# Attention's two shorter high halves of the probabilities: from ScalarE to GpSimd

## The reference

```python
x = x + 0.5 * _L0_ffn_ref(_layernorm(x), ...)
x = x + _L0_attn_ref(_layernorm(x), w_q, w_kv, w_dense)
x = x + 0.5 * _L0_ffn_ref(_layernorm(x), ...)
# _L0_attn_ref, the part that matters here:
scores = jnp.einsum('bqgpd,bkgd->bgqpk', q, k) * SCALE
scores = jnp.where(causal, scores, -jnp.inf)
probs = jax.nn.softmax(scores, axis=-1)
ctx = jnp.einsum('bgqpk,bkgd->bqgpd', probs, v)
return jnp.einsum('bse,eh->bsh', ctx, w_dense)
```

## Time and profile before

| | us |
|---|---|
| median of 3 runs | 2606.5 (2606.39 to 2609.38) |
| profiled execution | 2606.3 |
| its span | 2604.5 |
| TensorE busy in the span | 2512.5 (96%) |
| VectorE busy | 2151.8 (83%) |
| ScalarE busy | 945.6 (36%) |
| GpSimd busy | 909.6 (35%) |

### The profile page before, as it was taken

The page is one execution under the profiler, slowest core; times in us unless marked ns, Lnnn a source line. Parts: engine busy times, 40 slices in busy tenths (PEclk is TensorE's granted clock), DMA queues, the critical chain, the costliest instruction groups (busy, mean ns, idle before and its releaser), DMA issues. The chain is left out here.

```text
span 2604.5 us, 45222 instructions
## 1 busy us (share of the span) xinstructions
PE 2512.5 (96%) x14116; PEld 2298.7 (88%) x14116; DVE 2151.8 (83%) x6164; ACT 945.6 (36%) x2546; POOL 909.6 (35%) x1950
## 2 busy tenths in 40 slices
PE   6999999999997999999999999997999999999998
PEld 6999999999995888888888888886899999999997
DVE  6888888888886888888888888886888888888887
ACT  3111111101103777777777777774101101101100
POOL 4332332332323434343434344334332322323321
PEclk9999999999998999999999999998999999999999
DMA  6000000000001554554545554555000000000000
GB/s 191 13 1 1 1 1 1 1 1 1 1 25 50 91 91 92 92 92 92 89 90 88 90 92 92 89 96 136 25 9 1 9 9 1 9 9 1 9 9 9
DMA packets 378736, 117.25 MB, mean 45 GB/s; under 512 B 338561, under 2 KB 377473, under 8 KB 378497
## 3 DMA queue, kind: packets, MB, share of 16 engines
q1 hardware_dynamic: 378496, 114.36, 22.0%
HBM read 26.24 MB, written 4.19 MB: 12 GB/s over the span
## 5 line engine op out<-in xcount | busy, mean ns | idle before, releaser
L555 PE MATMUL ffn_ring<-ffn_mix_weights,ffn_yT 128*128 128x384 f32 x5760 | 1157.2, 342 | 5.9 <-DVE ffn_mix_weights L790 3.4
L555 PEld LDWEIGHTS ffn_ring<-ffn_mix_weights,ffn_yT 128*128 128x128 f32 x5760 | 1009.1, 190 | 56.7 <-DVE ffn_mix_sums L725 15.8
L727 DVE SCALAR_TENSOR_TENSOR ffn_mix_sums<-ffn_ring,ffn_w,ffn_mix_sums 128x384 f32<-128x384 f32 x896 | 550.6, 615 | 244.1 <-PE ffn_ring L555 227.5
L605 PE MATMUL ffn_ring<-ffn_out_weights,ffn_avT 128*128 128x512 f32 x1536 | 442.9, 399 | 6.3 <-POOL ffn_avT L1028 4.5
L1547 ACT ACTIVATE attn_exponentials<-attn_exponentials,attn_score_neg_max 128x512 f32<-128x512 f32 (+3 forms) x512 | 285.7, 559 | 164.3 <-DVE attn_score_neg_max L1462 163.7
L1615 POOL CAST attn_probsT_long<-attn_turned_long 128x1024 fp32r<-128x1024 f16 (+1 forms) x256 | 232.5, 936 | 251.1 <-DVE attn_probs L1479 250.4
L605 PEld LDWEIGHTS ffn_ring<-ffn_out_weights,ffn_avT 128*128 128x128 f32 x1536 | 283.0, 189 | 36.2 <-POOL ffn_avT L1028 5.7
L1479 DVE SCALAR_TENSOR_TENSOR attn_probs<-attn_exponentials,attn_prob_factor,attn_probs 128x512 f16<-128x512 f32 (+3 forms) x512 | 248.2, 546 | 15.5 <-ACT attn_probs L1556 15.2
L1556 ACT ACTIVATE attn_probs<-attn_exponentials,attn_prob_factor 128x512 f16<-128x512 f32 (+3 forms) x512 | 250.0, 552 | 23.1 <-DVE attn_prob_factor L1472 15.6
L742 DVE SCALAR_TENSOR_TENSOR x<-ffn_ring,ffn_w_out,x 128x256 f32<-128x256 f32 x512 | 247.1, 483 | 13.0 <-PE ffn_ring L605 6.5
L1302 PE MATMUL attn_scores<-attn_kT,attn_qT 128*128 128x512 f32 (+2 forms) x1152 | 242.8, 338 | 4.7 <-DVE attn_qT L1445 3.2
(11 more groups left out here) (149 smaller groups left out, 3262.4 us busy)
## 6 DMA issues: line engine op xcount, KB each, us to landing
ffn_mix_stage<-in_L_ffn_q_proj_dram SPq DMA_DIRECT2D x32, 128.0 KB, 2.5
ffn_mix_stage<-in_L_ffn_k_proj_dram SPq DMA_DIRECT2D x32, 128.0 KB, 2.5
ffn_mix_stage<-in_L_ffn_v_proj_dram SPq DMA_DIRECT2D x32, 128.0 KB, 2.8
ffn_out_stage<-in_L_ffn_o_proj_dram SPq DMA_DIRECT2D x16, 256.0 KB, 2.9
out_dram<-x SPq DMA_DIRECT2D x8, 512.0 KB, 2.9
x<-in_L_attn_x_dram SPq DMA_DIRECT2D x7, 512.0 KB, 8.3
early_stage<-in_L_attn_w_q_dram SPq DMA_DIRECT2D x4, 512.0 KB, 5.2
attn_dense_stage<-in_L_attn_w_dense_dram SPq DMA_DIRECT2D x4, 512.0 KB, 4.8
```

The costliest lines, as they stand in the source:

```text
L555: last = pe.matmul(bank[:, 0:QKV], yT[:, t % 2, h, k * P:(k + 1) * P], mix_half(e, wh)[:, k], start=(n == 0), stop=(n == 3 * CK - 1))
L605: last = pe.matmul(bank[:], avT[:, t % 2, h], wo[:, g, wh], start=(i == 0), stop=(i == 2))
L727: dve.scalar_tensor_tensor(into, bank[:, 0:QKV], w[:, t, e:e + 1], into, ALU.mult, ALU.add).then_inc(mix_done, 1)
```

## The change

GpSimd gets a function that makes the high halves of the blocks 1 and 0 of the unit before, and calls it at the head of its slot, ahead of its wait for the low halves and of its casts. ScalarE keeps the blocks 3 and 2. The semaphore that counted high halves becomes two, one for each engine, and VectorE's low halves wait for the one of their block. The wait for the landed short transpose goes to GpSimd together with the work.

```diff
-        p_hi, p_lo = sem("prob_hi"), sem("prob_lo")
+        p_hi_long, p_hi_short, p_lo = sem("prob_hi_long"), sem("prob_hi_short"), sem("prob_lo")
...
             def split_probs(u, i):
                 _, h, n = u
-                dve.wait_ge(p_hi, done_of(n, i))
+                dve.wait_ge(p_hi_long if pair_of(i) else p_hi_short, 2 * n + 2 - i % 2)
...
                 act.activation(prob_half(0, i), expo[:, at:at + width].rearrange("p (j k) -> p j k", k=P), ACT.Copy,
-                               scale=p_factor[:, h % 2, i:i + 1]).then_inc(p_hi, 1)
+                               scale=p_factor[:, h % 2, i:i + 1]).then_inc(p_hi_long, 1)
...
                 if prev:
-                    for i in reversed(range(QT)):
-                        split_probs(prev, i)
+                    split_probs(prev, 3)
+                    split_probs(prev, 2)
...
+            def split_short_probs(u, i):
+                _, h, n = u
+                pool.wait_ge(r_done, 4 * n + 4 - i // 2 * 2)
+
+                reach(pool, t_landed[pair_of(i)], 16 * n)
+                at, width = PROB_AT[i], (i + 1) * P
+                pool.tensor_scalar(prob_half(0, i), expo[:, at:at + width].rearrange("p (j k) -> p j k", k=P),
+                                   p_factor[:, h % 2, i:i + 1], None, ALU.mult).then_inc(p_hi_short, 1)
...
             def slot(b, h):
+                prev = unit(b, h, 1)
+                if prev:
+                    split_short_probs(prev, 1)
+                    split_short_probs(prev, 0)
```

## The result

The changed kernel takes 2660.7 us in the median of five runs (2654.96 to 2663.77) against 2606.4 us of the kernel before in the same session: a ratio of 1.0205, 95% interval 1.0194 to 1.0216. That is slower by 54 us where 31 were forecast. It lies inside the range of 2613 to 2666 us that the chances were given for, but above the 2618 to 2658 us that the forecast's own steps allowed, in the stretch that rival (a) claimed. The profiled execution took 2661.75 us, its span 2659.7.

The account below looks back on a forecast made before the run. TensorE was taken to bound the attention stage, VectorE second. ScalarE's relief counted nothing; VectorE's 0.45 us loss per head reached TensorE as 31 us, so 2606.3 + 31 = 2637 us, own range 2618 to 2658, overall 2613 to 2666.

Parts of the forecast that it names:

- (a): GpSimd kept out until VectorE's two long low halves are done; d of 0.6 to 0.8 us, 2650 to 2667 us; chance 0.17.
- Part 1: ScalarE losing two rows per head, about 0.8 us, only lengthens its idle time: worth nothing; upper bound 14.8 us.
- Part 2: GpSimd's two new operations at its slot's head take about 0.54 and 0.43 us, with their data in time.
- Part 3: GpSimd's reads collide with VectorE's two-input low halves; VectorE loses each operation's length less 0.25 us, d = 0.45 us.
- d: VectorE's loss per head in the attention stage: 0.45 us, low end 0.19, high end 0.70.
- Part 4: VectorE's lateness reaches TensorE at dense in slots without enough margin: 4.1 us per item, 31 us in all.
- (b): Port held for the whole of GpSimd's operation: d = 0.97 us, some 10 us per item, 2683 us; chance 0.03.
- (c): No difference: port holds so brief that margins and idle swallow them; 2606 us, 2603 to 2611; chance 0.09.
- (d): Faster: no real collision, ScalarE's relief brings forward high halves VectorE waits for; 8 us, 2598 us; chance 0.04.
- The signs that I gave: Low halves grow 0.45 us per head (384-wide and 128-wide); TensorE's wait 29 to about 60 us; ScalarE's up 0.8 us.

Follow-up runs that it names:

- e5: Changed kernel, but ScalarE keeps block 1 and GpSimd makes only block 0's high half (128 columns): 2616.2 us, 1.0038.
- e6: Changed kernel with GpSimd copying the exponentials instead of scaling them, factor left out of the short high halves: 2619.0 us, 1.0054.
- e2: Kernel before, ScalarE making all four high halves, plus GpSimd doing the two new operations into a buffer nobody reads: 2625.7 us, 1.0068.
- e9: Changed kernel with GpSimd filling the short high halves with zeros, three fills each, reading nothing from SBUF: 2656.4 us, 1.0189.
- e11: Changed kernel with GpSimd's layer norm power moved behind the two short high halves of the next slot: 2656.6 us, 1.0190.
- e4: Changed kernel with ScalarE also making the two short high halves, into a spare buffer: 2658.3 us, 1.0195.
- e10: Changed kernel with GpSimd filling the short high halves with zeros, five and three fills, no SBUF reads: 2744.3 us, 1.0528.
- e7: Changed kernel with VectorE's maxima of block 3 moved between its second and third low halves: 2632.8 us, 1.0101.
- e1: Kernel before with nobody making the two short high halves, so ScalarE is relieved and GpSimd gets nothing: 2606.05 us, 0.9997.
- e3: Kernel before with GpSimd making four constant fills of a spare buffer at the slot's head, reading nothing: 2607.0 us, 0.9998.
- e8: Kernel before, but ScalarE scales the two short blocks in place and GpSimd makes both their high and low halves: 2596.5 us, 0.9965.

## Why the prediction was right in kind and short in size

**One curve for these runs.** The time goes with the burst's mean length, whether the burst is lengthened by the port or by lateness:

```
run                 burst us  longer by  time us   more   us per us
e5 one block          2.073     0.133    2616.2    10.1      76
e6 copies             2.124     0.184    2619.0    12.8      70
e2 port alone         2.212     0.272    2625.7    19.7      72
e9 fills              2.488     0.548    2656.4    49.7      91
e11 power behind      2.512     0.572    2656.6    49.9      87
e4 ScalarE busy       2.522     0.582    2658.3    52.3      90
changed kernel        2.547     0.607    2660.7    54.3      89
e10 more fills        3.208     1.268    2744.3   137.7     109
```

e9 has no read in its high halves and costs about as much per us as e4 and e11: the changed kernel needs no large cause beyond its longer burst. The agreement is not a proof, because e9's lateness lies differently over the slots (3.3 us in slot 9, 2.2 in slots 1, 2 and 13). By the intervals e2's price is 49 to 81 us per us and the changed kernel's 83 to 93, so the price does rise; e5 and e6 are too uncertain to be ranked. e10's 109 contains the lower clock: less my estimate of 29 us it is 86, no more than the four runs at 0.55 to 0.61. (e7's burst has the maxima inside and can't be compared.)

**Part 1 (the relief is worth nothing): right,** e1 and e4.

**Part 2 (0.54 and 0.43 us, data in time): wrong,** the step that failed. Undisturbed the operations take 0.92 and 0.60 us. The slope between them, (922 - 602) / 128 = 2.5 ns per column, is three times that of the casts from which I had extrapolated. e6's copies of the same blocks (0.40 and 0.29 us) show that the operation makes the difference, not the data: a multiplication by a per-row scalar is not a cast. 0.92 us alone would still have been in time (e9, slots 3 and 5 to 8). What I left out is that the hold works both ways: I priced GpSimd's hold on VectorE, but "undisturbed" was wrong of GpSimd, which starts 0.18 us behind VectorE and loses some 0.42 us to its first low half. The earlier trace rows had that too, 1.11 us for 0.735. The sum, 0.18 + 1.35 = 1.53 us, passes the 1.2 us at which the third low half is due. Together with the overlap between instructions that a gap takes away, with slots 9 to 12 and with the four late transposes, this lateness makes the 0.607 of the changed kernel out of e2's 0.272.

**Part 3 (the collision, d = 0.45): mechanism right, its terms wrong, the sum in its range.** GpSimd did get in after the first of the back-to-back low halves in most heads. But VectorE did not lose GpSimd's duration less 0.25 us, which would be 0.67 and 0.35 us. It lost 0.22 us by the 256-wide operation and 0.11 by the 128-wide one: in the head at 1230 us, taken apart, the second low half lasts 830 instead of 612 ns and the third 585 instead of 478. d was 0.61: port 0.27 and lateness 0.33, in place of port 0.45. That the time came into the range is in part luck: the port was priced at 0.45 us instead of 0.27 and the lateness at nothing instead of 0.33, and the two errors go opposite ways. The port alone, rightly priced, would have given e2's 20 us.
The sentence of the Trainium skill, page "SBUF — State Buffer", section "Who interferes with whom", that the loser blocks for the whole instruction, does not hold here where VectorE is the loser: it lost 0.22 of 0.92 us, and its second low half in the head at 1230 us even ended 0.04 us before the GpSimd operation that it ran beside. Where GpSimd is the loser the trace agrees: it was kept out until VectorE's operation was over. Its other half, that only a GpSimd operation that reads SBUF contends with two-input VectorE work, agrees with e3 against e2.

**Part 4 (lateness to TensorE): the method right, its margins too generous.** With d = 0.607 its steps give 7 x 0.607 + 0.93 (slots 3 and 4) + 0.46 (7 and 8) + 0.18 (9 and 13) = 5.8 us per item, about 44 us in the proportion in which 4.1 gave 31; measured 54. So of the 23 us that the forecast missed, 13 are d and 10 are margins, with up to 5 us of lower clock among these 10. The rows above say which. Slot 1, said to absorb, waits 0.26; slots 3 and 4 take 0.65 and 0.81, together 1.46 where the steps give 0.93 (GpSimd was kept out in this head of slot 3). In slots 10 to 12 the waits grow by 0.5, 1.2 and 1.0 us in this item; in slots 11 and 12 the head is a kept-out one, 1.02 us longer than before. In slot 13, where VectorE waits for ScalarE first, the wait grows by 0.3 only. Slot 8 gave nothing, not 0.46: lateness of slot 7 did not add up there. The table shows the same: a burst up to 0.27 us longer costs some 70 us per us and one 0.6 us longer some 90, as more slots run out of margin; with every one of the 128 heads out of margin it would be 128.

**The rivals.** (a), GpSimd kept out for two low halves, is true of nine heads and of seven more behind the power; the new wait that it foretold is the line of 27 heads. Its time, 2650 to 2667, came true by another way: most heads are not kept out, but late. (b), (c) and (d) fall: to e2, to e5 (even one 128-wide operation costs 10 us), and to e1. The signs that I gave: the low halves grew by 0.27 us in sum instead of 0.45, and it was the 384-wide and 256-wide ones (150 and 84 ns), with 28 ns for the first and 3 for the last, where I had named the 384-wide and 128-wide ones. ScalarE's wait rose by 1.1 us per head instead of 0.8, TensorE's to 77 instead of 60, and the new wait for GpSimd, listed for (a), was there together with longer low halves, listed for the forecast. I had put them down as exclusive; they were two parts of one thing.

## What to carry to other kernels

When work is moved to an engine whose reads collide with a neighbour's (here GpSimd's with VectorE's), price the hold both ways: what the moved operation takes from its neighbour, and how late it ends itself when it must first wait for the neighbour. Then compare that end with the moment at which its result is due; here the margin was 0.1 us and the hold 0.4. And where the second engine is nearly as critical as the first, ask which whole instructions can leave it: moving a high half helped nobody, moving the low halves with it (e8) gave 10 us.

## What was not expected of the hardware

- A GpSimd multiplication by a per-row scalar took 922 ns for 256 columns and 602 for 128, against 401 and 290 for casts of such sizes and 0.40 and 0.29 us for e6's copies of the same blocks.
- It cost a two-input VectorE operation beside it 0.22 and 0.11 us, about 0.85 ns per column, 24% and 18% of the GpSimd operation's length; the copies cost 0.14 and 0.03. Fills cost nothing (e3). Why a copy costs less than a scaling of the same columns stays open.
- In the other direction VectorE's 512-wide low half held GpSimd until it was over. GpSimd operations that started 0.07, 0.18 and 0.53 us after it began lasted 1.47, 1.35 and 1.01 us, and all ended 1.53 to 1.55 us after that moment, 0.8 us after its end. Whether GpSimd then gets in behind the first low half or only behind the second differed between heads with the same order of instructions: 58 heads to nine without the power in front and 14 to seven with it in the changed kernel, three to four in slot 9 of e11. What decides it was not tried.
- After waits of 1.8 to 3.0 us TensorE's granted clock was at 1.2 instead of 2.4 GHz for 3.4 us, 20 times in e10's attention stage. A lateness of another engine can so cost more than the wait itself.
